# All sixteen heads' probabilities turned by VectorE and DMA for items 33 to 43, and scores placed ahead of values in the step

## The reference

```
x = x + attention(layernorm(x), layernorm(x)) @ w_ao          # phase A
x = x + attention(q from layernorm(x), k, v from ctx) @ w_co  # phase B
x = x + gelu(layernorm(x) @ w1) @ w2                          # the MLP
a = layernorm(ctx)
Q, K, V = x @ Wq.T, a @ Wk.T, a @ Wv.T                        # phase D
attn = softmax(where(mask, Q K^T / sqrt(32), -inf))
x = x + tanh(gate) * (attn V) @ Wo.T
```

## Time and profile before

| what | value |
|---|---|
| median of three runs | 1102.0 us (1101.92 to 1104.04) |
| span of the profiled execution | 1100.7 us |
| what lies around the span, median less span | 1.3 us |
| busy: PE, DVE, ACT, POOL | 98%, 74%, 65%, 42% |
| granted TensorE clock | full speed |
| DMA | 167.04 MB, mean 152 GB/s, 47.9% of 16 engines' span |
| step 34 to 44 of phase D, first exponentials to first exponentials | 905.7 to 1051.8 us |

### The profile page before, as it was taken

One profiled execution on the slowest core, in us unless ns is written; L12 is line 12 of the kernel. 1 busy time (PEld: TensorE's weight loads), 2 busy tenths in 40 slices (PEclk: granted clock), 3 DMA queues, 4 the chain that ended last, 5 costly groups with the idle time before them and its releaser, 6 DMA issues.

```text
span 1100.7 us, 24328 instructions
## 1 busy us (share of the span) xinstructions
PE 1074.7 (98%) x8829; PEld 934.2 (85%) x8829; DVE 815.4 (74%) x1314; ACT 712.7 (65%) x2365; POOL 462.0 (42%) x337
## 2 busy tenths in 40 slices
PE   7989999999999999998999999999999999999998
PEld 6888888888888888886898888888888988888886
DVE  6678787778888778888877557656677478778777
ACT  4678777777788778786444434434444387777776
POOL 3665666557767776767512121103012331122100
PEclk9999999999999999999999999999999999999999
DMA  6366565576776777553241130220622146666633
GB/s 216 98 201 198 191 195 188 174 227 216 221 227 215 223 211 229 180 191 128 85 134 40 38 96 12 85 96 1 181 101 83 59 146 205 203 198 210 177 97 97
DMA packets 136135, 167.04 MB, mean 152 GB/s; under 512 B 16992, under 2 KB 82256, under 8 KB 136016
## 3 DMA queue, kind: packets, MB, share of 16 engines
q1 hardware_dynamic: 136016, 165.50, 47.9%
HBM read 113.15 MB, written 52.29 MB: 150 GB/s over the span
## 4 chain that ended last, share of the span: by engine, by line
PE 59%; DVE 12%; ACT 9%; POOL 7%; issue 4%; DMA 3%; SPq 1%; DVEq 0%; ACTq 0%; POOLq 0%
PE psum L938 15%; PE psum L919 14%; PE psum L758 13%; POOL prob L2023 6%; PE psum L858 5%; PE psum L750 5%; ACT prob L1217 4%; ACT prob_blocks L1217 2%; PE psum L794 2%; PE psum L776 2%; DVE prob L1590 2%; DVE ln_tile L1528 2%; PE psum L835 2%; DVE negmax L1603 2%; ACT inputs_transposed L1255 2%
## 5 line engine op out<-in xcount | busy, mean ns | idle before, releaser
L758 PE MATMUL psum<-inputs_hi,weights_hi 128*128 128x256 f32 x768 | 223.7, 291 | 5.4 <-POOL inputs_lo L2014 2.5
L758 PE MATMUL psum<-inputs_lo,weights_hi 128*128 128x256 f32 x768 | 217.1, 283 | 0.0
L758 PE MATMUL psum<-inputs_hi,weights_lo 128*128 128x256 f32 x768 | 217.0, 283 | 0.0
L2014 POOL TENSOR_TENSOR inputs_lo<-inputs_transposed,inputs_hi 128x512 fp32r<-128x512 f32 x84 | 113.0, 1367 | 228.9 <-DVE inputs_hi L1563 168.4
L2023 POOL TENSOR_TENSOR prob<-prob,mask_bias 128x1024 f32<-128x1024 f32 x64 | 152.7, 2408 | 98.3 <-DVE prob L1590 96.3
L1217 ACT ACTIVATE prob<-prob,negmax 128x128 f32<-128x128 f32 x472 | 182.2, 391 | 0.5 <-DVE negmax L1603 0.5
L758 PEld LDWEIGHTS psum<-inputs_hi,weights_hi 128*128 128x128 f32 x768 | 146.7, 191 | 10.3 <-issue 2.8
L1603 DVE TENSOR_REDUCE negmax<-prob 128x8 f32<-128x1024 f32 x96 | 115.9, 1210 | 50.0 <-POOL prob L2023 50.0
L758 PEld LDWEIGHTS psum<-inputs_lo,weights_hi 128*128 128x128 f32 x768 | 147.0, 191 | 0.2
L758 PEld LDWEIGHTS psum<-inputs_hi,weights_lo 128*128 128x128 f32 x768 | 146.9, 191 | 0.0
L858 PE MATMUL psum<-weights_hi,context_parts 128*128 128x512 f32 x376 | 125.8, 393 | 0.4 <-ACT kT L1168 0.3
(11 more groups left out here) (124 smaller groups left out, 2600.3 us busy)
## 6 DMA issues: line engine op xcount, KB each, us to landing
prob_turned<-prob_blocks SPq DMA_DIRECT2D x37, 512.0 KB, 3.0
prob<-prob_turned SPq DMA_DIRECT2D x148, 128.0 KB, 3.3
weights_whole<-weights_in SPq DMA_DIRECT2D x72, 256.0 KB, 3.4
normalised<-ln_tile SPq DMA_DIRECT2D x30, 512.0 KB, 2.8
inputs_transposed<-normalised SPq DMA_DIRECT2D x120, 128.0 KB, 2.9
context<-row_sums_spread SPq DMA_DIRECT2D x188, 64.0 KB, 2.1
stream<-residual SPq DMA_DIRECT2D x42, 256.0 KB, 2.7
residual<-stream SPq DMA_DIRECT2D x42, 256.0 KB, 3.7
```

Source lines behind the costliest of these rows:

```text
L758: mm = pe.matmul(ps[:, bank, GT * part:GT * part + GT], w[:, slot, c, o], a[:, buf, c, :], start=c == 0 and i == 0, stop=c == KC - 1 and i ...
L2014: pool.tensor_tensor(lo, y, hi.bitcast(f32), ALU.subtract).then_inc(s_rlo if fill.ln is None else s_flo, 1)
```

## The change

`WHOLE` is the tuple of items 33 to 43. For them all sixteen heads are turned by DVE: quarters 2 and 3 have a second tile, `second_prob_blocks`, a second DVE transpose, and an exchange through DRAM of their own, issued from ACT's queue. PE's transposes and ACT's `probs_out` of these items are gone. In steps 35 to 45 `times_v(g-2)` stands behind `scores(g)`. The row sums of these items use PSUM bank T_BANK + 1 in place of U_BANK + 1. DVE takes mask bias and the first masked half before the context of the older item where that is one of these. The low part of the context (`context_lo`) of items 32 to 43 moves from DVE to POOL.

```
+WHOLE = tuple(range(33, 44))
+LO_BY_POOL = tuple(range(32, 44))
 def row_sum_bank(g):
-    return U_BANK if sums_late(g) else U_BANK + 1
+    return T_BANK + 1 if g in WHOLE else U_BANK if sums_late(g) else U_BANK + 1
...
 # PE, row_sums
-                if sums_late(g):
+                if g in WHOLE:
+                    pe.wait_ge(s_cx, 2 * g)
+                elif sums_late(g):
...
 # PE, times_v
-                pe.wait_ge(s_pta, copied_by_act(g, 1))
+                if g in WHOLE:
+                    pe.wait_ge(s_rc, g + 1)
+                    pe.wait_ge(s_moved2, 64 * second_number(g))
+                else:
+                    pe.wait_ge(s_pta, copied_by_act(g, 1))
...
 # PE, step
-                if st.ends:
+                if st.ends and g - 2 not in WHOLE:
                     times_v(g - 2)
...
                     scores(g)
+                if g - 2 in WHOLE:
+                    times_v(g - 2)
...
-                    else:
+                    elif g - 1 not in WHOLE:
                         transpose_prob(g - 1, 2)
                         if g != 44:
                             transpose_prob(g - 1, 3)
                 if not late:
-                    if st.prev:
+                    if g - 1 in WHOLE:
+                        u_bank_free(g)
+                    elif st.prev:
                         row_sums_out(g - 1)
                     project(*st.units[1], U_BANK + 1)
...
 # ACT, exps
+                second = g in WHOLE and quarter >= 2
+                if second and quarter == 2 and second_number(g) > 1:
+                    act.wait_ge(s_pst2, 16 * (second_number(g) - 1))
...
+            def store_second_blocks(g):
+                n = second_number(g)
+                act.wait_ge(s_turned2, n)
+                if n > 2:
+                    act.wait_ge(s_moved2, 64 * (n - 2))
+                act.dma_start(turned_second[n % 2], second_blocks[:, :]).then_inc(s_pst2, 16)
+
+            def bring_second_blocks(g):
+                n = second_number(g)
+                act.wait_ge(s_pst2, 16 * n)
+                blocks = turned_second[n % 2].rearrange("(i k) (j n) -> j k i n", i=4, j=4)
+                for j in range(4):
+                    dst = prob[32 * j:32 * j + 32, g % 2, NH // 2 * T:].rearrange("p (i n) -> p i n", i=4)
+                    act.dma_start(dst, blocks[j]).then_inc(s_moved2, 16)
...
 # ACT, step
-                elif st.prev and g != 44:
+                elif st.prev and g != 44 and g - 1 not in WHOLE:
                     probs_out(g - 1)
+                if g - 1 in WHOLE:
+                    store_second_blocks(g - 1)
...
                 if not st.ends:
                     half_out(*st.units[2])
+                if g - 1 in WHOLE:
+                    bring_second_blocks(g - 1)
                 if g != 28:
                     exps(g, 0)
...
 # DVE
+            def turn_second_blocks(g):
+
+                dve.wait_ge(s_exp, 4 * g + 4)
+                dve.transpose(second_blocks[:, :], second_blocks[:, :]).then_inc(s_turned2, 1)
...
-                late = st.ends and sums_late(g - 2)
+                late = st.ends and (sums_late(g - 2) or g - 2 in WHOLE)
...
                     inverse_sums(g - 1)
+                if g - 1 in WHOLE and late:
+                    turn_second_blocks(g - 1)
                 mask_scores(g, 1)
-                if late:
+                if late and g - 2 not in LO_BY_POOL:
                     context_lo(g - 2, 0)
                     context_lo(g - 2, 1)
...
 # POOL
+            def context_lo(g, h):
+                half = slice(256 * h, 256 * h + 256)
+                pool.wait_ge(s_chi, 2 * g + h + 1)
+                pool.tensor_tensor(clo[0][:, half], ctxn[:, half], chi[0][:, half].bitcast(f32), ALU.subtract).then_inc(s_clo, 1)
...
+                if g - 2 in LO_BY_POOL:
+                    context_lo(g - 2, 0)
+                    context_lo(g - 2, 1)
```

More of the change, by code:

```diff
@@ L151, with second_number, turned_by_pe @@
 BY_PE = (0, 27, 28, 29, 30, 31, 32, 44, 45, 46, 47)
+WHOLE = tuple(range(33, 44))
+LO_BY_POOL = tuple(range(32, 44))
 def moved_number(g):
     return g + 1 - sum(k <= g for k in BY_PE)
+def second_number(g):
+    return sum(k <= g for k in WHOLE)
+def turned_by_pe(k):
+    return 4 if k in BY_PE else 0 if k in WHOLE else 2
 def transposed_count(g, c):
-    return sum(4 if k in BY_PE else 2 for k in range(g)) + (c + 1 if g in BY_PE else c - 1)
+    return sum(turned_by_pe(k) for k in range(g)) + (c + 1 if g in BY_PE else c - 1)
 def copied_by_act(g, half):
-    return sum(2 if k in BY_PE else 1 for k in range(g)) + (half + 1 if g in BY_PE else 1)
+    return sum(turned_by_pe(k) // 2 for k in range(g)) + (half + 1 if g in BY_PE else 1)
 def copied_by_dve(g, half):
@@ L297, in build @@
         turned = nc.dram_tensor("prob_turned", (2, 128, NH // 2 * T), f32, kind="Internal").ap()
+        turned_second = nc.dram_tensor("second_prob_turned", (2, 128, NH // 2 * T), f32, kind="Internal").ap()
         spread = nc.dram_tensor("row_sums_spread", (4, KC * T), f32, kind="Internal").ap()
@@ L319, in build @@
         s_moved = sem("prob_blocks_moved")
+        s_pst2 = sem("second_prob_blocks_stored")
+        s_moved2 = sem("second_prob_blocks_moved")
         s_scores = sem("scores")
@@ L362, in build @@
         s_turned = sem("prob_blocks_turned")
+        s_turned2 = sem("second_prob_blocks_turned")
         s_clo = sem("ctx_lo")
@@ L813, in row_sums_out, with u_bank_free @@
                 pe.wait_ge(s_rc, g + 1)
+            def u_bank_free(g):
+                if g - 1 in (1, 33):
+                    half_out(g // 16, 1, 4)
+                else:
+                    stream_out(g - 3)
             def times_v(g):
                 phase, q, gp, half = g // 16, (g % 16) // 2, (g // 2) % 2, g % 2
-                pe.wait_ge(s_pta, copied_by_act(g, 1))
+                if g in WHOLE:
+                    pe.wait_ge(s_rc, g + 1)
+                    pe.wait_ge(s_moved2, 64 * second_number(g))
+                else:
+                    pe.wait_ge(s_pta, copied_by_act(g, 1))
                 if g in BY_PE:
@@ L831, in times_v @@
                         P = prob[:, g % 2, T * h:T * h + T]
-                        if h < NH // 2 and g not in BY_PE:
-                            P = by_head(prob[:, g % 2, 0:NH // 2 * T])[:, h]
+                        if (h < NH // 2 and g not in BY_PE) or g in WHOLE:
+                            eight = h // 8 * NH // 2 * T
+                            P = by_head(prob[:, g % 2, eight:eight + NH // 2 * T])[:, h % 8]
                             out = out.rearrange("p (i q) -> p i q", q=32)
@@ L984, in step @@
                 if not late:
-                    if st.prev:
+                    if g - 1 in WHOLE:
+                        u_bank_free(g)
+                    elif st.prev:
                         row_sums_out(g - 1)
                     project(*st.units[1], U_BANK + 1)
-                if g == 44:
+                if g == 44 and g - 1 not in WHOLE:
                     transpose_prob(g - 1, 3)
@@ L1214, in exps @@
                     dst = src
-                    if moved:
-                        dst, src = by_head(pblocks[:, :])[:, s], src.rearrange("p (j k) -> p j k", k=32)
+                    if moved or second:
+                        blocks = second_blocks if second else pblocks
+                        dst, src = by_head(blocks[:, :])[:, s % 8], src.rearrange("p (j k) -> p j k", k=32)
                     ins = act.activation(dst, src, ACT.Exp,
@@ L1718, in step @@
                     inverse_sums(g - 1)
+                if g - 1 in WHOLE and not late:
+                    turn_second_blocks(g - 1)
+                if st.ends and not late and g - 2 not in LO_BY_POOL:
                     context_lo(g - 2, 0)
```

2 lines of the change are left out of this document (added).

## The result

The changed kernel takes 1128.3 us (1123.4 to 1133.6) against 1102.9 for the kernel before on the same chip: ratio 1.0234, 95% interval 1.0201 to 1.0267. It is slower, as forecast, by 25 us where 6 were forecast and 1118 was the end of the range. The profiled execution is the shortest of the four, 1123.4 us with a span of 1122.0, so the trace explains 21.3 of the 25 us.

What follows compares the result with a forecast made beforehand. PE, 98% busy, was taken as the bound; the change would close a 14.96 us loop through ACT's queue. 11 L - 37.9 at L = 4.0 gives +6.1 on 1100.7, plus 1.3: 1108 us, range 1096 to 1118.

Steps and rivals of the forecast that it cites:

- the loop of the forecast: Item to item through ACT's queue, DVE's transposes and the second store's landing, without PE: 14.96 us a step.
- The tail: After item 44's first exponential, item 43's values wait for their blocks: 1.0 us more.
- Rival (a): PE stays the pace, the loop being under 13.8 us a step: 1094 to 1095 us, chance 0.2.
- Edge: Entry to the changed stretch: item 34's exponentials start at 907.27, 1.55 us later than before.
- L: Time from ACT's second store to its landing, for which the four loads wait: taken as 4.0 us.
- the loaded row: Landing of other 512 KB stores, issued with more in flight, in the kernel before: 3.9 us.
- DVE's 4.44 us: Loop part on DVE from `turn_blocks` through `inverse_sums`, said to stay at 4.44 us despite reordering.
- Rival (d): DMA engines choke, L at 4.9 and issues at 3.1 us: +28, 1130 us, chance 0.1.
- At nothing: Scores before values, low parts on POOL and row sums in another bank were forecast to cost nothing.

Runs made afterwards that it cites:

- e_all: Changed kernel with the previous item's blocks loaded, one plain load, third half unit copied first, a quarter of the second exchange's bytes: 1103.3 us, 1.0008.
- the idle exchange: Kernel before, plus a store and four loads of unused tiles issued by ACT in steps 34 to 44, all bytes, no landing wait: 1119.7 us, 1.0159.
- the last version: e_all with the third half unit copied where the changed kernel copies it and values ahead of scores again: 1103.5 us, 1.0015.

## Why the prediction was right or wrong

**Right.** PE no longer sets the pace, and the loop of the forecast does: three of its five parts have the forecast's length within 0.04 us, and none has slack. Four issues and what follows them take 2.00 us, where SP's row gave 1.96; the first exponential to `turn_blocks` takes 3.22 against 3.21. The tail is 1.0 later, as said. Rival (a) fell: with all known obstacles gone the best was a tie. The 8.5 us of idle time ahead of the row sums in that run (e_all) fit the 8.7 of the removed transposes; a kernel that is faster by them was not seen.

**Edge.** Item 34 was to start 1.55 later and started 1.57 earlier: its mask rows had landed 3.0 us earlier (DVE takes them at 894.31, before at 897.32). This is 3.1 us in the change's favour, and luck.

**The failed step: two terms of the loop.** The first is L, taken at 4.0 beside the loaded row; it measured 4.93 in the ten steps, and 4.84 over all eleven stores (4.02 to 6.00). The second is DVE's 4.44 us, with "the same instructions, so the sum stands", and with it the sentence that one item's exponentials hang on the item's before "without PE". It measured 5.26, since the mask in it waits for the values of item g-2, these stand behind the scores, and the scores of every second item wait for q, which ACT copies out behind the exponentials. The account closes: +6.1 forecast, +9.3 from L, +8.2 from DVE's part, +0.8 from the small parts, -3.1 at the edge is +21.3, the difference of the two spans.

**What made L long: the price of the traffic.** The forecast noted 276 GB/s asked and 242 at 85%, and then charged it to a single landing. With a quarter of the bytes L is 3.96. All other landings were left as they were, and the idle exchange shows what this omits: 18.7 us slower without any loop through ACT. In the changed kernel this does not add to the loop, it stands right behind it, as cutting the loop shows (3 us). Rival (d), "the DMA engines choke", had the right total, 1130, at a chance of 0.1, and the right L, 4.9; the other half of its sum was wrong, as the issues stayed at 2 us.

The estimate by the Trainium skill, "DMA: Bandwidth & Descriptors", section "Anatomy of one DMA", was 3.2 us for 512 KB. The trace of after disagrees for ACT's store, 4.9, and agrees for SP's, 3.0.

**"At nothing."** The swap was put there because DVE masks late. The question asked was when the scores are needed; the one that counted was when their inputs are ready. It costs 3.7 us on the kernel before, and nothing that can be told in the changed one, where the values wait instead.

**Open.** How the 15 us of the bytes divide over SP's landings: the layernorm tiles carry some 5, within the noise. Which ring holds the last version at 14.7 us a step; its chain names SP's queue, but that was not tested. And the low parts on POOL and the row sums' other bank were never run alone: that they cost nothing, as the forecast had it, is not shown.

## What to carry to other kernels

When DMA engines are two thirds busy and several queues work in order, price added traffic by what it does to every landing that a queue waits for, not by its own transfer alone; a copy of the traffic tied to nothing is the experiment that shows it in one run. Where one engine is 98% busy, don't take what is removed from it as gain: here, with every known obstacle gone, a step stayed at 14.7 us where the engine alone would need 13.8. When one follows a loop from item to item, the waits that protect a shared buffer belong to it: here the mask waited for the values that it overwrites. When two groups of work change places, look up when the inputs of the one that goes first are ready.

## What was not expected of the hardware

- The DMAs did not slow down alike. From the kernel before (DMA share 0.65 in its ten steps) to the one with the idle exchange (0.81), the median landing of the layernorm tiles went from 4.2 to 6.3 us and that of the residuals from 3.4 to 5.2, but that of SP's own 512 KB store from 3.3 to 3.0. Traffic is not all of it: with the swap alone and no byte more, the tiles landed in 5.1 us.
- Pieces of 1 KB or rows of 4 KB in the loads made no difference that could be told (1.0159 and 1.0191).
- Around PE's restart after idle times of 3.6 and 3.9 us the mean granted clock was 0.79 (924 to 932 us) and 0.72 (1024 to 1030 us); keeping PE at work through such times won 3 us, within the noise.
